# Layer-norm sums on another engine, and quantization units spread over two stages, in a transformer layer on 8 cores

## The reference

```python
x = x + attn(layernorm(x), w_qkv, b_qkv, w_out, b_out)   # 16 heads of 128, causal softmax
x = x + ffn(layernorm(x), w1, b1, w2, b2)

def layernorm(x):                       # over the last axis, 2048 values
    return (x - mean(x)) / sqrt(var(x) + 1e-5)

def ffn(x):                             # w1 is 8192 x 2048, w2 is 2048 x 8192
    q = lambda w: sign(w) * (abs(w) >= 0.7 * mean(abs(w)))
    return gelu(x @ q(w1).T + b1) @ q(w2).T + b2
```

## Time and profile before

| | |
|---|---|
| median of 3 runs | 3721.32 us (3705.62 to 3721.9) |
| the profiled execution | 3703.43 us |
| its span on the slowest core | 3701.8 us (all cores: 3677.7 to 3701.8) |
| TensorE busy | 1903.7 us, 51% of the span |
| VectorE busy | 1073.1 us, 29% |
| ScalarE busy | 784.0 us, 21% |

### The profile page before, as it was taken

One profiled execution on the slowest core, in us unless ns is written; L12 is line 12 of the kernel. 1 busy time (PEld: TensorE's weight loads), 2 busy tenths in 40 slices (PEclk: granted clock), 3 DMA queues, 4 the chain that ended last, 5 costly groups with the idle time before them and its releaser, 6 DMA issues.

```text
span 3701.8 us, 29444 instructions; the slowest of 8 cores (3677.7 to 3701.8 us)
## 1 busy us (share of the span) xinstructions
PE 1903.7 (51%) x10418; PEld 985.2 (27%) x10418; DVE 1073.1 (29%) x1714; ACT 784.0 (21%) x1024; POOL 187.7 (5%) x329
## 2 busy tenths in 40 slices
PE   0013445667899422212212210443019999999999
PEld 0001112223677012212212200221004444444444
DVE  4400000000232555555554550444301112211122
ACT  3424554555000422212212200000140100011000
POOL 0000000000000001111111111121000000000000
PEclk9996777888999556656656655776559999999999
DMA  4498887888311345565565569775732435344352
GB/s 128 165 198 269 259 259 250 257 256 262 128 48 40 111 138 167 175 209 168 177 216 166 189 216 223 179 177 149 163 79 46 82 55 91 61 76 80 57 91 91
DMA packets 513313, 569.33 MB, mean 154 GB/s; under 512 B 353296, under 2 KB 410640, under 8 KB 508944
## 3 DMA queue, kind: packets, MB, share of 16 engines
q1 hardware_dynamic: 389072, 433.13, 43.0%
q0 software_dynamic: 30016, 75.58, 6.4%
q10 hardware_dynamic: 94080, 58.73, 6.4%
HBM read 387.00 MB, written 104.86 MB: 133 GB/s over the span
## 4 chain that ended last, share of the span: by engine, by line
PE 41%; DMA 26%; DVE 11%; ACT 7%; issue 6%; ACTq 4%; SPq 3%; DVEq 0%; POOL 0%; POOLq 0%
DMA p1buf<-w 20%; PE psA L1138 12%; PE psB L1154 6%; PE psA L1154 6%; PE psA L437 3%; PE psB L437 3%; DVE evq L650 3%; DMA w2q_hbm<-evq 2%; DVE evq L647 2%; ACT p1buf L492 2%; ACTq L927 2%; ACTq L320 2%; PE psA L982 2%; PE psB L982 2%; PE psA L748 2%
## 5 line engine op out<-in xcount | busy, mean ns | idle before, releaser
L1138 PE MATMUL psA<-C,B 128*128 128x512 bf16 x2048 | 451.3, 384 | 194.5 <-DMA C<-x2ln_hbm 175.3
L417 PE MATMUL psA<-A,C 128*128 128x512 bf16 x768 | 200.9, 430 | 558.0 <-DMA A<-xln_hbm 243.4
L748 PE MATMUL psA<-B,C 128*128 128x129 bf16 x640 | 104.4, 246 | 623.3 <-DVE C L894 623.3
L492 ACT ACTIVATE p1buf<-p1buf 128x1024 f32<-128x1024 f32 x256 | 270.2, 1056 | 321.3 <-DMA p1buf<-w 309.5
L1138 PEld LDWEIGHTS psA<-C,B 128*128 128x128 bf16 x2048 | 201.8, 99 | 444.0 <-issue 208.8
L1173 DVE TENSOR_TENSOR A<-psB,A 128x512 f32<-128x512 f32 x128 | 79.5, 683 | 662.4 <-PE psB L1154 550.2
L417 PEld LDWEIGHTS psA<-A,C 128*128 128x128 bf16 x768 | 81.8, 108 | 676.6 <-issue 608.8
L1080 ACT ACTIVATE C<-psA,b1cols 128x512 bf16<-128x512 f32 x128 | 81.1, 685 | 788.7 <-PE psA L1138 788.7
L748 PEld LDWEIGHTS psA<-B,C 128*128 128x128 bf16 x640 | 70.7, 111 | 640.9 <-issue 639.0
L454 DVE CAST C<-C 128x4096 bf16<-128x4096 f32 x16 | 36.7, 2294 | 688.4 <-DMA C<-wqkv 688.4
L1154 PE MATMUL psB<-B,C 128*128 128x512 bf16 x1024 | 226.2, 379 | 13.0 <-ACT C L1080 13.0
(11 more groups left out here) (159 smaller groups left out, 2062.8 us busy)
## 6 DMA issues: line engine op xcount, KB each, us to landing
p1buf<-w SPq DMA_DIRECT2D x512, 512.0 KB, 5.7
C<-wqkv SPq DMA_DIRECT2D x96, 512.0 KB, 7.4
w1q_hbm<-evq POOLq DMA_DIRECT2D x80, 256.0 KB, 4.6
w2q_hbm<-evq POOLq DMA_DIRECT2D x80, 256.0 KB, 5.1
C<-xg SPq DMA_DIRECT2D x16, 1024.0 KB, 7.2
w1q_hbm<-C POOLq DMA_DIRECT2D x48, 256.0 KB, 5.5
w2q_hbm<-C POOLq DMA_DIRECT2D x48, 256.0 KB, 5.3
xln_hbm<-C ACTq DMA_DIRECT2D x16, 512.0 KB, 7.0
```

What stands on the lines that cost most here:

```text
L417: inst = t.matmul(ps[:, t4 * 512:(t4 + 1) * 512], lhs, xlnv(dc)[:, t4 * 512:(t4 + 1) * 512], start=(dc == 0), stop=(dc == 15))
L492: X.bump("cS", s.activation(out=p1s[u % 3], in_=p1s[u % 3], func=AF.Abs, accum_out=pacc[:, lu:lu + 1]))
L748: inst = t.matmul(pav[:, 1536:1665], PTv[par][:, u * 256 + qt * 128:u * 256 + qt * 128 + 128], vslot(h, s_), start=(pos == 0), stop=(pos = ...
L1138: inst = t.matmul(psA[:, bank * 512:(bank + 1) * 512], lhs, x2lnfm(dc)[:, t2 * 512:(t2 + 1) * 512], start=(dc == 0), stop=(dc == 15))
```

## The change

It has two parts. In LN1 the two sums of a tile are taken by ScalarE, with an `Identity` and a `Square` activation that accumulate along the row, as LN2 does, and no longer by VectorE. ScalarE waits for the variance of the tile before, since both sums go to one place in `statc`; its wait for the store of tile `i-2` stands ahead of the normalization. In the projection one unit stands behind each eviction instead of two, and four units stand behind each LN2 tile. GpSimd's spills between the weight loads are eight instead of 16.

```diff
@@ p1_sync
                     X.wait(q, f"ln1_norm_{i-2}")
-                    X.wait(q, f"ln1_r0_{i-2}")
@@ p1_scalar
                 X.wait(s, f"ln1_ld_{i}")
-                if i >= 2:
-                    X.wait(s, f"ln1_sp_{i-2}")
-                    X.wait(s, f"ln1_r2_{i-2}")
-                X.bump("cS", s.square(out=sqf[i % 2], in_=xt[i % 2]))
-                X.mark(f"ln1_sq_{i}", "cS")
+                if i >= 1:
+                    X.wait(s, f"ln1_var_{i-1}")
+                X.chain(s, "cS", s.activation(out=sqf[i % 2], in_=xt[i % 2], func=AF.Identity,
+                                              accum_out=statc[:, LN_S0:LN_S0 + 1]))
+                X.bump("cS", s.activation(out=sqf[i % 2], in_=xt[i % 2], func=AF.Square,
+                                          accum_out=statc[:, LN_S2:LN_S2 + 1]))
+                X.mark(f"ln1_sums_{i}", "cS")
...
                 X.wait(s, f"ln1_nmr_{i}")
+                if i >= 2:
+                    X.wait(s, f"ln1_sp_{i-2}")
@@ p1_vec
-                X.wait(v, f"ln1_ld_{i}")
-                if i >= 1:
-                    X.wait(v, f"ln1_norm_{i-1}")
-                X.chain(v, "cV", v.tensor_reduce(out=statc[:, LN_S0:LN_S0 + 1], in_=xt[i % 2],
-                                                 axis=AX.X, op=ALU.add))
-                X.mark(f"ln1_r0_{i}", "cV")
-                X.wait(v, f"ln1_sq_{i}")
-                X.chain(v, "cV", v.tensor_reduce(out=statc[:, LN_S2:LN_S2 + 1], in_=sqf[i % 2],
-                                                 axis=AX.X, op=ALU.add))
-                X.mark(f"ln1_r2_{i}", "cV")
+                X.wait(v, f"ln1_sums_{i}")
@@ p4_pool
                 if db >= 1:
-                    qsp_issue(gp, 16)
+                    qsp_issue(gp, 8)
@@ p4_vec
                     X.mark(f"op_ev_{u}", "cV")
-                    quant(v, 2)
+                    quant(v, 1)
@@ p5_vec
                 X.mark(f"ln2_nmr_{i}", "cV")
+                quant(v, 4)
```

## The result

The changed kernel takes 3656.8 us at the median (9 runs), the one before 3718.0 us (10 runs); the ratio is 0.9857, with a 95% interval from 0.9822 to 0.9892. That is 40 to 66 us less, 53 in the middle. Both kernels have some runs far above their median (up to 3813 and 3886 us) with a lower granted clock on some cores; the ratio leaves these out. The forecast was 3640, the range 3612 to 3674.

The account below looks back on a forecast made before the run. Bound taken: the `evq` round trip pacing VectorE's units, for which TensorE waits. Terms: -8.5 - 75.8 - 29.7 + 6.3 + 31.8 + 4 = -71.9 us, giving 3631.5 (profiled) or 3649 (median); forecast 3640, range 3612 to 3674.

Parts of the forecast that it names:

- LN1 (at the first matmul): LN1: sums on ScalarE start the first statistics 4.85 us earlier and shorten the other tiles; 8.5 us less in all.
- three waits for evictions: Projection blocks 0 to 2: the last eviction follows the 7th unit, not the 14th; TensorE waits 75.8 us less.
- last block to the first LN2 statistic: Last projection block: VectorE has 8 units instead of 16 ahead of LN2's first statistics; 29.7 us less.
- LN2, seven tiles: LN2: four units behind each tile lengthen the first by 6.3 us and six more by 31.8 us.
- transposes of x2ln: Transposed loads behind LN2: three spills and a load beside their start slow them, costing 4 us.
- these statistics come 29.7 us earlier: LN2's first statistics, on VectorE: they wait for ScalarE's sums at 2635.5 instead of all 16 units until 2665.19.
- cover of about 4 us: Last projection block: VectorE finishes its 8th unit about 4 us before ScalarE's sums for LN2's first tile.
- at the pace of the blocks: LN2: two round trips of 7.0 us, as in the projection blocks, make a tile at least 14.0 us; 14.3 taken.
- 147.3 us for 21 pairs: Projection: TensorE's three waits divided by 21 pairs of units, taken as 7.0 us a round trip of an `evq` half.
- the second rival: LN2's spills are slower than the blocks': tiles of 18 to 24 us, kernel 3666 to 3708 us; chance 0.14.
- low bound of 11.0 us: LN2 tile if a spill lands in 2.3 us, so that `evq` holds VectorE up only once a tile.
- the low end: Spill landing in LN2, without TensorE's weight loads, would be near 2.3 us of the 2.3 to 9.7 us spread.

Follow-up runs that it names:

- e4: The changed kernel with all 64 last units moved into the feed-forward stage, none behind evictions or in LN2; 3514.1 us, ratio 0.9472 to the kernel before.
- e5: The changed kernel with four output buffers for LN2's units instead of the two halves of `evq`; 3629.6 us, ratio 0.9785 to the kernel before.
- e6: The changed kernel without the weight loads of LN2's 32 units; no kernel time given, LN2 tile 12.2 to 12.4 us, spill landing 2.5 to 2.8 us.
- e7: The changed kernel without the stores of normalized LN2 tiles 1 to 6, eight stores made earlier instead; no kernel time given, LN2 tile 15.6 us.
- e3: The changed kernel with LN2's 32 units moved to the first four feed-forward groups, eight each; ratio 0.9726 to the kernel before.

## Why the prediction was right, and where its sizes were off

The direction, the mechanism and the range held. The size did not: the sum was 72 us, and the result, 53, has an interval (40 to 66) that ends below it. The forecast of 3640 lies 17 us below the 3656.8; the two wrong steps, 27 us together, are less than half of the range's 62. By its own steps, in means over eight cores:

| step | predicted | measured |
|---|---|---|
| LN1 (at the first matmul) | -8.5 | -9.2 |
| three waits for evictions | -75.8 | -78.6 |
| last block to the first LN2 statistic | -29.7 | -16.5 |
| LN2, seven tiles | +38.1 | 7 x 7.3 = +51.3 |
| transposes of x2ln | +4 | +2.6 |
| sum | -71.9 | -50.4 |

The feed-forward start moved by 47.5 us and not by 50.4: of LN1's 9.2 us, 6.9 are left at the projection's first matmul, and LN2's last store lands later, so that from the last bias to the transposes it is 6.6 us instead of 5.4, a term that the prediction put at nothing.

- The three waits came out as read. The argument that the pace belongs to the unit and not to what stands between, so that half the units means half the wait, is what e2 (the placement alone) shows, and e4 (all 64 units moved on) drives it to its end: without units 10.9 us are left.
- LN1 is right in size and confirmed by e1 (LN1's part alone) in the trace. Its first part is visible as one instant: the first statistic at 24.17 instead of 29.16.
- The step "these statistics come 29.7 us earlier" is 13 us too large. I had taken it from core 3 in the one execution shown, where the block's first eviction stood 82.6 us before the statistic. That core was the extreme of its eight (68.3 to 82.6, mean 72.6). I priced the slowest core, since it sets the time. But its rows hold its own bad luck, which the slowest core of another execution doesn't repeat; by the means 23.5 us were to be had there (72.6 - 44.9 - 4.2), which is 6 of the 13. The other 7 us are the w2 transposes: ScalarE's sums begin 51.9 us behind the first eviction where it was 44.9. Over all kernels with units in that block the mean lies between 43.0 and 51.9, and the two kernels with two units behind each eviction have 44.9 and 48.3, so this may be scatter; it stays open. The cover of about 4 us between the eighth unit and the sums did hold: on every core the first statistic follows the start of the sums by the same 4.2 us.
- The step "at the pace of the blocks" is the second: 14.3 us a tile taken, 16.3 measured, 14 us over the seven tiles. The mechanism is right, as e5 (four buffers, 12.5 us) and e6 (no loads, 12.3 us) show from two sides. The size is off first because the blocks' pace was misread: "147.3 us for 21 pairs" counts seven round trips in a block where there are six, so the trip was 7.6 us and not 7.0 (0.9 us a tile). Then LN2 is not the blocks: its stores join, as the second rival had it (0.7 us, e7), and 0.4 us stay open. The low bound of 11.0 us for a spill landing in 2.3 us was too low by 1.3: e6 has 12.3 at 2.5. For the three waits the misreading did no harm, since there the price came from the very instants of the seventh unit.
- The Trainium skill, "DMA: Bandwidth & Descriptors", section "Latency and other measured facts", has the latency of HBM rise with load. I had held that by this rule LN2 would lie towards the low end. The landing of a spill moves in the rule's direction in e6 (2.5 us without the loads, 5.7 with them); whether it is HBM that is loaded or the DMA engines, no run here tells apart. My application was the wrong way round: the traffic beside a spill in LN2 is the units' own, not TensorE's.
- What neither the sum nor a rival had: the units need not be paid for anywhere ahead of the feed-forward stage. The change moved half of them from one critical place to another, which gave 79 + 16 us and took back 51; e3 and e4 show what it is worth to move them off that path.

## What to carry to other kernels

Work that fills an idle engine costs its pace, not its busy time, wherever another engine waits behind it in that queue. Find that pace (here the round trip of a double buffer, 7.2 to 8.5 us for a pair of units that works for 4.1 us) before moving it, and count how many trips really wait, since the first use of each half waits for none. Then move it to a stage that is bound by something else, with its loads and in the order of its deadlines, rather than to a neighbour on the same path. Price a step from several cores and not from the slowest one.

## What the runs showed of the hardware

The landing time of the same 256 KB spill ranges from 2.5 us with no loads beside it through 4.5 us in a block of the projection and 5.7 us in LN2 to 9.7 us beside transposes, so a double buffer's round trip is a property of the stage. The eight w2 transposes are issued in 20 to 24 us, by core, without units beside them (e4), and in 39 to 46 us with them in the kernel before. And the feed-forward stage took 64 units, 48 MB of loads and spills, without getting longer (880 us on core 6, 877 before), at a DMA share of 0.58.
